# When the expert loads are issued, how many result tiles there are, and which weights are loaded early, in a mixture-of-experts tail

## The chip, the cores and the metric

The kernel runs on one NeuronCore of a Trainium2 chip. The metric is the time of one execution on the device in microseconds (us). The median of three timed runs of the kernel before is 1958.4 us (1953.89 to 1959.58).

## What is computed

Sixteen sequences of 256 rows of 512 numbers go through four residual stages: a cross attention, a base matrix product with low-rank experts, a second attention with 8 heads, and last a mixture of 64 experts with the 8 best experts for each row and a capacity of 256 rows for each expert. The change touches the last stage:

```python
logits = xf @ router_weight
probs = jax.nn.softmax(logits.astype(jnp.float32), axis=-1)
topw, topi = jax.lax.top_k(probs, TOPK)
topw = topw / topw.sum(axis=-1, keepdims=True)
...
xe = jnp.zeros((E, CAP, d), x.dtype).at[se, pos].set(xf[tok], mode='drop')
h = jax.nn.silu(jnp.einsum('ecd,edi->eci', xe, gate_proj)) * jnp.einsum('ecd,edi->eci', xe, up_proj)
ye = jnp.einsum('eci,eid->ecd', h, down_proj)
contrib = jnp.where(valid[:, None], ye[se, posc], 0.0) * flat_w[order][:, None]
out = jnp.zeros((m, d), x.dtype).at[tok].add(contrib)
```

## The kernel before

The program has two parts. In the first, a written-out order interleaves the attention stages of the 16 sequences on all engines; at its end each row of a sequence is sent by GpSimd's indirect DMAs (line 1405) to the slots of its experts in a DRAM array, `slot_rows`, 128 rows and one of the 8 choices at a time. The first part ends when the last of these sends has landed.

In the second part the 64 experts are worked through, each in two units of 128 slots. Unit u belongs to expert u // 2. All engines walk over the same index t, each with its own lead:

- TensorE at t: transposes of the slot rows of unit t + 3 (line 762), the gate and up products of unit t + 2 (lines 773 to 775), the transposes of the hidden values of unit t + 1 (line 784), the down product of unit t (lines 795 to 797). Every product is made of three, from high and low parts of its factors.
- ScalarE at t: the high part of the transposed rows (line 988), silu (994), the high part of the hidden values (1000), the scaled result of unit t into the tile `y_slots` (`ye`, line 1008, in `down`), then half of an expert's `gate_up_hi` (1018) three experts ahead.
- VectorE at t: the low parts (lines 1300, 1314, 1321) and at even t the high part of the down weights, two experts ahead (1331).
- GpSimd: at odd t `add_rows(t // 2)`, two indirect DMAs (line 1454) that add the two result tiles of an expert to their rows of `out_rows` in DRAM; at even t `split_down((t + 4) // 2)`, the low part of an expert's down weights (line 1444). `add_rows(e)` waits until the additions of expert e - 1 have landed, since two experts may add to the same row.
- SyncE (SP) issues the loads: `load_weights(e)` (`gate_up`, 768 KB, and `down`, 384 KB, lines 493 and 496) and `load_rows(e)` (`x_slots`, 577 KB, line 504). There are five buffers (NB) of weights and of rows. `load_rows(e)` for e of 5 or more waits until the additions of expert e - 5 have landed, since these read their row numbers from the same buffer. In its main loop SP issues, for expert e, the weights of expert e + 4 and then the rows of expert e + 3.

There are two result tiles, one for each parity of the expert, so `down` of expert e waits until the additions of expert e - 2 have landed. The semaphores `added` count 32 for each expert. In GpSimd's order `split_down(e + 3)`, which raises `dn_lo_ok` to e + 4, stands directly behind `add_rows(e)`.

Of the kernel before, what the change touches and what calls it, by code (L numbers as in the profile page):

```python
# [7 lines left out]
ALU = mybir.AluOpType  # L8
ACT = mybir.ActivationFunctionType
# [6 lines left out]
P = 128  # L16
# [118 lines left out]
def build(nc, a, out, slots_dram, dims):  # L135
    B, HALF, T, L, NHEAD, DQ, NE, NEXP, CAP, TOPK, NRANK = (
        dims[k] for k in ("B", "HALF", "T", "L", "NHEAD", "DQ", "NE", "NEXP", "CAP", "TOPK", "NRANK"))
# [14 lines left out]
    NX = 4  # L152
    NB = 5
    NW = 3
    BC = NHEAD * C

    tensor_order = schedule(dims, TENSOR, TENSOR_TAIL, TENSOR_MAX, TENSOR_OUT, ("key", "score", "weighted"))
# [12 lines left out]
    for _, ev in tensor_order:  # L170
        stage = bank_stage(ev)
        if stage and stage not in use:
            i = min((read_last[i], taken[i], i) for i in range(3))[2]
            use[stage] = 5 + i, taken[i]
            taken[i] += 1
            read_last[i] = read_at[stage]

    stack = ExitStack()
    with stack:
        def sem(name):  # L180
            return stack.enter_context(nc.semaphore(name))

        def sb(name, shape, dt=F32, on=stack):
            return on.enter_context(nc.sbuf_tensor(name, shape, dt))

        psum = [stack.enter_context(nc.psum_tensor(f"bank{i}", [P, 512], F32)) for i in range(8)]
# [12 lines left out]
        sent = [sem(f"sent{i}") for i in range(2)]  # L199
# [52 lines left out]
        added = [sem(f"added{i}") for i in range(2)]  # L252
# [4 lines left out]
        dn_lo_ok = sem("dn_lo_ok")  # L257
# [101 lines left out]
        xe = [sb(f"x_slots{i}", [P, 2, ROW]) for i in range(NB)]  # L359
        gu_hi, gu_lo = ([sb(f"gate_up_{part}{i}", [P, C, 2 * INNER], F32R) for i in range(NW)] for part in ("hi", "lo"))  # L360
        dn_hi, dn_lo = ([sb(f"down_{part}{i}", [IC, 2, T], F32R) for i in range(NW)] for part in ("hi", "lo"))
        xt_hi, xt_lo = ([sb(f"x_slots_t_{part}{i}", [P, C, P], F32R) for i in range(3)] for part in ("hi", "lo"))
        act_g = [sb(f"silu{i}", [P, INNER]) for i in range(2)]
        hid = [sb(f"hidden{i}", [P, INNER]) for i in range(2)]
        ht_hi, ht_lo = ([sb(f"hidden_t_{part}{i}", [IC, 2, P], F32R) for i in range(2)] for part in ("hi", "lo"))
        ye = [sb(f"y_slots{i}", [P, 2, T]) for i in range(2)]


        N_WEIGHTS = 16 * (3 * HALF + 10)
# [2 lines left out]
        U = 2 * NEXP  # L372

        full_a = [BC * B // 2] * 4 + [0] + taken

        def sent_before(b):

            return 16 * HALF * TOPK * (b // 2)
# [4 lines left out]
        def expert_slots(e_):  # L383
            return slots_dram[e_ * CAP:(e_ + 1) * CAP, :].rearrange("(c p) w -> p c w", p=P)
# [4 lines left out]
        def _(e):  # L389
            w = Waits(e)  # L390
# [31 lines left out]
            def stacks_free(b):  # L422
                if b >= 2:
                    n = BC * (b - 1)
                    w.wait_ge(full[0], n // 2)
# [63 lines left out]
            def load_weights(e_):  # L489
                i, k = e_ % NB, e_ // NB  # L490
                if k:
                    w.wait_ge(gu_lo_ok, 2 * (e_ - NB) + 2)
                e.dma_start(gu[i][:, :, :], a["gate_up"][e_]).then_inc(weights_of[i], 16)
                if k:
                    w.wait_ge(dn_lo_ok, e_ - NB + 1)
                e.dma_start(dn[i][:, :, :], a["down"][e_]).then_inc(weights_of[i], 16)

            def load_rows(e_):
                i, k = e_ % NB, e_ // NB
                if k:  # L500
                    u = 2 * (e_ - NB) + 1
                    w.wait_ge(free[6 + u % 2], full_a[6 + u % 2] + u // 2 + 1)
                    w.wait_ge(added[(e_ - NB) % 2], 32 * ((e_ - NB) // 2 + 1))
                e.dma_start(xe[i][:, :, :], expert_slots(e_)).then_inc(rows_of[i], 16)

            load_weights(0)
            for i in range(2):
                w.wait_ge(sent[i], sent_before(B))
            for e_ in range(NB - 2):
                load_rows(e_)  # L510
                load_weights(e_ + 1)
            for t in range(0, U, 2):
                if t // 2 + NB - 1 < NEXP:
                    load_weights(t // 2 + NB - 1)
                if t // 2 + NB - 2 < NEXP:
                    load_rows(t // 2 + NB - 2)
            for i in range(2):
                w.wait_ge(added[i], 32 * (NEXP // 2))
            w.wait_ge(slots_filled, 16 * (NEXP + 1))
# [2 lines left out]
        def _(e):  # L522
            w = Waits(e)

            def take(bank, n):

                if n:
                    w.wait_ge(free[bank], n)
# [109 lines left out]
            def score_chunk(n):  # L638
                b, head, c, h = place(n)
                take(2 + n % 2, n // 2)  # L640
                if n % BC == 0:
                    w.wait_ge(q_in[b % 2], 16 * 3 * HPH * (b // 2 + 1))
# [59 lines left out]
            def dispatch(b, what, _):  # L702
                if what in ("x0", "x1"):
                    k = int(what[1])
                    w.wait_ge(rows_ok, 2 * b + k + 1)
                    bank, done = turn_of("disp", what, b)
                    for c in range(C):
                        m = e.transpose(bank[:, c * P:(c + 1) * P], rows[b % 2][:, k, c * P:(c + 1) * P], ident[:, :])
                    m.then_inc(done, 1)
                elif what == "route":  # L710
                    for k in range(HALF):
                        bank, n = use["disp", f"x{k}", b]
                        w.wait_ge(free[bank], n + 1)
                    bank, done = turn_of("disp", what, b)
                    for k in range(HALF):
                        for c in range(C):
                            m = e.matmul(bank[:, k * NEXP:(k + 1) * NEXP], x_t4[:, k, c, :], route_w[:, c, :],
                                         start=c == 0, stop=c == C - 1)
                    m.then_inc(done, 1)
                elif what == "place":  # L720
                    w.wait_ge(mask_ok, b + 1)
                    if b:
                        w.wait_ge(seen_ok, b)
                    bank, done = turn_of("disp", what, b)
                    for k in range(HALF):
                        dst = bank[:, k * NEXP:(k + 1) * NEXP]
                        e.matmul(dst, below[:, :], mask[:, k, :], start=True, stop=False)
                        for kk in range(k):
                            e.matmul(dst, ones[:, :], mask[:, kk, :], start=False, stop=False)
                        m = e.matmul(dst, ones[:, :], seen[:, :], start=False, stop=True)  # L730
                    m.then_inc(done, 1)
# [33 lines left out]
            def up(u):  # L765
                e_ = u // 2
                nw = e_ % NW
                bk = psum[2 + u % 2]
# [18 lines left out]
            def down(u):  # L787
                e_ = u // 2
                nw = e_ % NW
                bk = psum[6 + u % 2]  # L790
# [20 lines left out]
        def _(e):  # L811
            w = Waits(e)
# [190 lines left out]
            def down(u):  # L1003
                e_, s = divmod(u, 2)
                w.wait_ge(full[6 + u % 2], full_a[6 + u % 2] + u // 2 + 1)
                if e_ >= 2:
                    w.wait_ge(added[e_ % 2], 32 * (e_ // 2))
                e.activation(ye[e_ % 2][:, s, :], psum[6 + u % 2][:, :], ACT.Copy,  # L1008
                             scale=xe[e_ % NB][:, s, T + 1 + e_:T + 2 + e_]).then_inc(free[6 + u % 2], 1)

            def split_gate_up(e_, half):
                i, nw = e_ % NB, e_ % NW
                cs = slice(half * C // 2, (half + 1) * C // 2)
                w.wait_ge(weights_of[i], 32 * (e_ // NB + 1))
                if e_ >= NW:
                    u = 2 * (e_ - NW) + 1
                    w.wait_ge(full[2 + u % 2], full_a[2 + u % 2] + u // 2 + 1)
                e.copy(gu_hi[nw][:, cs, :], gu[i][:, cs, :]).then_inc(gu_hi_ok, 1)  # L1018
# [14 lines left out]
        def _(e):  # L1033
            w = Waits(e)
# [255 lines left out]
                    dispatch(*ev[1:])  # L1290

            w.wait_ge(slots_ok, B)
            for i in range(2):
                w.wait_ge(sent[i], sent_before(B))

            def turn(u):
                w.wait_ge(xt_hi_ok, u + 1)
# [48 lines left out]
        def _(e):  # L1346
            w = Waits(e)
# [99 lines left out]
            def add_rows(e_):  # L1447
                i, u = e_ % NB, 2 * e_
                w.wait_ge(free[6], full_a[6] + e_ + 1)
                w.wait_ge(free[7], full_a[7] + e_ + 1)  # L1450
                if e_:
                    w.wait_ge(added[(e_ - 1) % 2], 32 * ((e_ - 1) // 2 + 1))
                for q in range(2):
                    e.indirect_dma_start(  # L1454
                        out=out, out_offset=bass.IndirectOffsetOnAxis(ap=xe[i][:, q, T:T + 1].bitcast(U32), axis=0),
                        in_=ye[e_ % 2][:, q, :], in_offset=None, compute_op=ALU.add).then_inc(added[e_ % 2], 16)

            for t in range(-6, U):
                if t >= 0 and t % 2:
# [48 lines left out]
```

## Time and profile before

| | |
|---|---|
| median of the timed runs | 1958.4 us |
| the profiled execution | 1951.5 us |
| its span | 1949.6 us |
| last send issued | 1278.6 us into the span |
| first additions issued by GpSimd | 1306.8 us |
| last expert's additions issued | 1941.8 us |
| TensorE busy, whole span | 86% |
| VectorE, ScalarE, GpSimd busy | 61%, 51%, 47% |

The span counts from the first instruction to the last one of the profiled execution. A row of the timeline gives start, duration, engine, line, operation and tiles, and in brackets how long the engine had stood idle before and what released it. A wait for several things is put down to the one that the profile saw last, so that a name in brackets can be wrong where two things end close together.

### The profile page before, as it was taken

What the parts mean: (1) busy time and instruction counts of PE and PEld (TensorE: products, weight loads), DVE (VectorE), ACT (ScalarE), POOL (GpSimd) and SP (SyncE); (2) the same over time, 40 slices, a digit from 0 to 9 for tenths busy, and PEclk for the clock granted to TensorE, in tenths of its full rate; (3) what the DMA queues carried; (4) which work ended last, traced back from release to release, by engine and by line L of the source; (5) the groups of instructions that cost most, each with busy time, mean ns of one, the idle gap of its engine ahead of it and who ended that gap; (6) DMA issues with size and microseconds to landing.
All of it is one profiled execution on the core that took longest, in us unless ns stands there. A gap on an engine that the chain in (4) does not pass through costs nothing.

```text
span 1949.6 us, 25985 instructions
## 1 busy us (share of the span) xinstructions
PE 1678.9 (86%) x8672; PEld 1086.1 (56%) x8672; DVE 1195.8 (61%) x2644; ACT 996.1 (51%) x1970; POOL 922.4 (47%) x880
## 2 busy tenths in 40 slices
PE   4688999999999999999999988459888888888885
PEld 2343454544554544555455443258777777777775
DVE  2465677777777777677777765346555555554553
ACT  3345656656655655655665635135444444444443
POOL 1121225445446436436535536645555555555555
PEclk9889999999999999999999989679999999999998
DMA  9767325345344343332332220168888888888885
GB/s 335 241 232 250 87 53 165 107 137 162 106 141 140 113 112 115 103 104 80 95 87 71 58 65 25 37 219 230 225 216 227 233 227 223 215 229 225 222 222 89
DMA packets 138194, 303.31 MB, mean 156 GB/s; under 512 B 26617, under 2 KB 27513, under 8 KB 138062
## 3 DMA queue, kind: packets, MB, share of 16 engines
q1 hardware_dynamic: 99150, 230.23, 39.1%
q0 software_dynamic: 38912, 71.43, 15.3%
q8 instruction: 69, 1.13, 0.2%
q14 instruction: 63, 0.52, 0.1%
HBM read 132.60 MB, written 155.91 MB: 148 GB/s over the span
## 4 chain that ended last, share of the span: by engine, by line
PE 37%; DMA 25%; POOL 14%; DVE 9%; issue 7%; ACT 5%; SPq 3%; POOLq 0%; ACTq 0%
DMA out_rows<-y_slots,x_slots 23%; POOL out_rows L1454 5%; POOL slot_rows L1405 5%; PE bank L652 5%; PE bank L644 4%; PE bank L665 4%; PE bank L625 4%; POOL p_sum L1393 3%; PE bank L688 3%; ACT y_slots L1008 2%; SPq L410 2%; PE bank L598 2%; PE bank L566 2%; PE bank L681 2%; PE bank L612 1%
## 5 line engine op out<-in xcount | busy, mean ns | idle before, releaser
L1174 DVE TENSOR_REDUCE max_col<-bank 128x1 f32<-128x512 f32 x512 | 345.4, 684 | 216.2 <-PE bank L644 213.7
L929 ACT ACTIVATE p_t<-bank 128x512 f32<-128x512 f32 x512 | 298.2, 597 | 283.2 <-PE bank L652 264.0
L1405 POOL DMA_INDIRECT slot_rows<-row,slot_i x256 | 266.5, 1041 | 330.3 <-DVE slot_i L1273 261.6
L1454 POOL DMA_INDIRECT out_rows<-y_slots,x_slots x128 | 201.1, 1571 | 291.1 <-ACT y_slots L1008 260.4
L652 PE MATMUL bank<-q_stack,k_stack 98*128 98x512 f32 x512 | 275.7, 540 | 5.5 <-ACT p_t L929 5.1
L773 PE MATMUL bank<-gate_up_hi,x_slots_t_hi 128*128 128x384 f32 x512 | 187.4, 366 | 87.3 <-DVE x_slots_t_lo L1300 87.2
L1300 DVE TENSOR_TENSOR x_slots_t_lo<-bank,x_slots_t_hi 128x512 fp32r<-128x512 f32 x128 | 88.5, 691 | 251.2 <-ACT x_slots_t_hi L988 244.7
L644 PE MATMUL bank<-k_stack,q_stack 96*128 96x512 f32 x512 | 216.0, 424 | 19.2 <-DMA q_stack<-xn 16.5
L1393 POOL TENSOR_TENSOR p_sum<-p_t 128x512 f32<-128x512 f32 x128 | 162.6, 1278 | 139.5 <-ACT p_t L929 138.4
L1008 ACT ACTIVATE y_slots<-bank,x_slots 128x512 f32<-128x512 f32 x128 | 88.7, 694 | 268.7 <-DMA out_rows<-y_slots,x_slots 257.6
L1444 POOL TENSOR_TENSOR down_lo<-down,down_hi 96x1024 fp32r<-96x1024 f32 x64 | 188.6, 2947 | 18.2 <-DVE down_hi L1331 18.2
L775 PE MATMUL bank<-gate_up_hi,x_slots_t_lo 128*128 128x384 f32 x512 | 176.2, 344 | 0.0
L774 PE MATMUL bank<-gate_up_lo,x_slots_t_hi 128*128 128x384 f32 x512 | 175.3, 342 | 0.0
L652 PEld LDWEIGHTS bank<-q_stack,k_stack 98*128 98x128 f32 x512 | 98.4, 193 | 133.2 <-issue 107.0
L1321 DVE TENSOR_TENSOR gate_up_lo<-gate_up,gate_up_hi 128x768 fp32r<-128x768 f32 x128 | 149.6, 1170 | 23.7 <-DMA slot_rows<-row,slot_i 23.7
L773 PEld LDWEIGHTS bank<-gate_up_hi,x_slots_t_hi 128*128 128x128 f32 x512 | 98.6, 193 | 100.8 <-DVE x_slots_t_lo L1300 100.5
L665 PE MATMUL bank<-p_t,v_t 128*32 128x512 f32 x1024 | 139.5, 617 | 0.0
L644 PEld LDWEIGHTS bank<-k_stack,q_stack 96*128 96x128 f32 x512 | 100.5, 197 | 60.1 <-DMA q_stack<-xn 24.1
L625 PE MATMUL bank<-base_w,x_t 128*128 128x512 f32 x256 | 126.7, 608 | 0.0
L1018 ACT CAST gate_up_hi<-gate_up 128x768 fp32r<-128x768 f32 x128 | 106.3, 831 | 36.3 <-DMA down<-in_down 36.3
L795 PE MATMUL bank<-down_hi,hidden_t_hi 96*128 96x512 f32 x256 | 113.6, 444 | 0.0
L762 PE MATMUL bank<-ident,x_slots 128*128 128x128 f32 x512 | 77.7, 274 | 29.7 <-DMA x_slots<-slot_rows 29.7
(174 smaller groups left out, 3269.1 us busy)
## 6 DMA issues: line engine op xcount, KB each, us to landing
gate_up<-in_gate_up SPq DMA_DIRECT2D x64, 768.0 KB, 5.7
slot_rows<-row SPq DMA_DIRECT2D x64, 577.0 KB, 8.6
x_slots<-slot_rows SPq DMA_DIRECT2D x64, 577.0 KB, 3.9
k_stack<-prob SPq DMA_DIRECT2D x192, 128.0 KB, 2.4
down<-in_down SPq DMA_DIRECT2D x64, 384.0 KB, 7.3
q_stack<-x_t SPq DMA_DIRECT2D x128, 128.0 KB, 2.3
x<-in_x SPq DMA_DIRECT2D x16, 512.0 KB, 4.2
ctx<-in_ctx SPq DMA_DIRECT2D x16, 512.0 KB, 3.8
```

The costliest lines, as they stand in the source:

```text
L625: e.matmul(bank[:, :], x_t[:, k, c, :], base_w[:, c, :], start=c == 0, stop=False)
L644: e.matmul(psum[2 + n % 2][:, :], q_st[b % 2][0:SK, head, c * P:(c + 1) * P], k_st[b % 2][0:SK, head, :], start=True, stop=True).then_inc( ...
L652: e.matmul(psum[n % 2][:, :], k_st[b % 2][0:SKM, head, j * P:(j + 1) * P], q_st[b % 2][0:SKM, head, :], start=True, stop=True).then_inc(fu ...
L665: m = e.matmul(psum[4][h * DQ:(h + 1) * DQ, :], v_t[b % 3][:, j, head + h, :], p_t[step % 2][:, h, :], start=j == 0, stop=j == C - 1)
L773: e.matmul(bk[:, 0:2 * INNER], xt_hi[u % 3][:, c, :], gu_hi[nw][:, c, :], start=c == 0, stop=False)
L775: m = e.matmul(bk[:, 0:2 * INNER], xt_lo[u % 3][:, c, :], gu_hi[nw][:, c, :], start=False, stop=c == C - 1)
L929: e.activation(p_t[step % 2][:, h, :], psum[n % 2][:, :], ACT.Exp, scale=SCALE).then_inc(free[n % 2], 1)
L1174: e.tensor_reduce(max_col[quad % 2][:, c, h:h + 1], psum[2 + n % 2][:, :], X, ALU.max, negate=True).then_inc(free[2 + n % 2], 1)
L1393: e.tensor_tensor(p_sum[:, h, :], p_t[(step - 1) % 2][:, h, :], p_t[step % 2][:, h, :], ALU.add).then_inc(p_sum_ok, 1)
L1405: e.indirect_dma_start(out=slots_dram, in_=rows[b % 2][:, k, :], in_offset=None, out_offset=bass.IndirectOffsetOnAxis(ap=slot_i[b % 2][:, ...
L1444: e.tensor_tensor(dn_lo[nw][:, :, :], dn[i][:, :, :], dn_hi[nw][:, :, :].bitcast(F32), ALU.subtract).then_inc(dn_lo_ok, 1)
L1454: e.indirect_dma_start(out=out, out_offset=bass.IndirectOffsetOnAxis(ap=xe[i][:, q, T:T + 1].bitcast(U32), axis=0), in_=ye[e_ % 2][:, q, : ...
```

## The change

There are three result tiles instead of two, so `down` of expert e waits for the additions of expert e - 3. SP loads the weights of experts 0 to 4 before it waits for the last sends (before: of expert 0 alone), then the rows of experts 0 to 3. In its main loop it waits, for expert e, until `dn_lo_ok` is e + 4, which GpSimd signals at the end of the `split_down` that stands behind `add_rows(e)`; only then it issues the weights of expert e + 5 and the rows of expert e + 4. VectorE no longer waits for the last sends before its work on the experts.

```diff
+    NY = 3
...
-        ye = [sb(f"y_slots{i}", [P, 2, T]) for i in range(2)]
+        ye = [sb(f"y_slots{i}", [P, 2, T]) for i in range(NY)]
...
-            load_weights(0)
+            for e_ in range(NB):
+                load_weights(e_)
             for i in range(2):
                 w.wait_ge(sent[i], sent_before(B))
-            for e_ in range(NB - 2):
+            for e_ in range(NB - 1):
                 load_rows(e_)
-                load_weights(e_ + 1)
-            for t in range(0, U, 2):
-                if t // 2 + NB - 1 < NEXP:
-                    load_weights(t // 2 + NB - 1)
-                if t // 2 + NB - 2 < NEXP:
-                    load_rows(t // 2 + NB - 2)
+            for e_ in range(NEXP):
+                w.wait_ge(dn_lo_ok, min(e_ + NB - 1, NEXP))
+                if e_ + NB < NEXP:
+                    load_weights(e_ + NB)
+                if e_ + NB - 1 < NEXP:
+                    load_rows(e_ + NB - 1)
...
-                if e_ >= 2:
-                    w.wait_ge(added[e_ % 2], 32 * (e_ // 2))
-                e.activation(ye[e_ % 2][:, s, :], psum[6 + u % 2][:, :], ACT.Copy,
+                if e_ >= NY:
+                    w.wait_ge(added[(e_ - NY) % 2], 32 * ((e_ - NY) // 2 + 1))
+                e.activation(ye[e_ % NY][:, s, :], psum[6 + u % 2][:, :], ACT.Copy,
...
             w.wait_ge(slots_ok, B)
-            for i in range(2):
-                w.wait_ge(sent[i], sent_before(B))
...
-                        in_=ye[e_ % 2][:, q, :], in_offset=None, compute_op=ALU.add).then_inc(added[e_ % 2], 16)
+                        in_=ye[e_ % NY][:, q, :], in_offset=None, compute_op=ALU.add).then_inc(added[e_ % 2], 16)
```

The program of the SyncE queue at the start of the second part, before. `gate_up` and `down` are an expert's weights, `x_slots` its rows, `sent0` and `sent1` the landing of the sends.

```order
L493 DMA gate_up<-in_gate_up 128x1536 [waits out_in1,out_in2,out_in0,out_in3,out_rstd_ok,slots_ok]
L496 DMA down<-in_down 96x1024
L504 DMA x_slots<-slot_rows 128x2x577 [waits sent1,sent0]
L493 DMA gate_up<-in_gate_up 128x1536
L496 DMA down<-in_down 96x1024
L504 DMA x_slots<-slot_rows 128x2x577
L493 DMA gate_up<-in_gate_up 128x1536
```

The same place of the changed kernel, whose lines are numbered one higher.

```order
L497 DMA down<-in_down 96x1024
L494 DMA gate_up<-in_gate_up 128x1536
L497 DMA down<-in_down 96x1024
L505 DMA x_slots<-slot_rows 128x2x577 [waits sent1,sent0]
L505 DMA x_slots<-slot_rows 128x2x577 x3
L494 DMA gate_up<-in_gate_up 128x1536 [waits gu_lo_ok,dn_lo_ok]
L497 DMA down<-in_down 96x1024
L505 DMA x_slots<-slot_rows 128x2x577
```

Ten weight loads now stand ahead of the wait for the sends, four row loads directly behind it, and the fifth row load stands behind a wait on `dn_lo_ok`.

The SyncE queue in the main loop, before: the weights wait for their buffer, the rows for the additions of five experts earlier.

```order
L493 DMA gate_up<-in_gate_up 128x1536 [waits gu_lo_ok]
L496 DMA down<-in_down 96x1024 [waits dn_lo_ok]
L504 DMA x_slots<-slot_rows 128x2x577 [waits added1,bank_free7]
L493 DMA gate_up<-in_gate_up 128x1536 [waits gu_lo_ok]
L496 DMA down<-in_down 96x1024 [waits dn_lo_ok]
```

And in the changed kernel.

```order
L494 DMA gate_up<-in_gate_up 128x1536 [waits gu_lo_ok,dn_lo_ok]
L497 DMA down<-in_down 96x1024
L505 DMA x_slots<-slot_rows 128x2x577 [waits added0,bank_free7]
L494 DMA gate_up<-in_gate_up 128x1536 [waits gu_lo_ok,dn_lo_ok]
L497 DMA down<-in_down 96x1024
```

Before, the wait that holds the queue stands at the rows, and the weights follow it freely. Now it stands at the weights, with a higher value of `dn_lo_ok` than the buffer needs, and the rows are the last of the three.

## Rows read from the trace of the kernel before

**Rows 1.** Busy time by stretch: start:end, length, engines, PEclk (granted clock), DMA share, GB/s.

```profile
1264.00:1278.00 14.00, 0.00 (x0) 0.00 (x0) 0.00 (x0) 0.96 (x2) 10.65 (x12) 0.50 0.04 5
...
1500.00:1600.00 100.00, 82.50 (x467) 73.55 (x467) 53.45 (x90) 47.50 (x100) 55.37 (x30) 1.00 0.83 227
1700.00:1800.00 100.00, 89.21 (x470) 79.57 (x468) 49.82 (x87) 46.00 (x96) 52.69 (x29) 0.93 0.82 220
```

**Rows 2.** Waits from 1340 to 1890: engine, line, releaser, us in total, times, longest.

```profile
ACT y_slots L1008 <- DMA out_rows<-y_slots,x_slots: 238.7, 54, 5.9
...
PE bank L773 <- DVE x_slots_t_lo L1300: 79.6, 47, 3.1
```

**Rows 3.** Timeline of one expert from 1499.9 us.

```profile
1499.90 0.38 SPq L504 DMA_DIRECT2D x_slots<-slot_rows  x1
1500.62 1.55 POOL L1454 DMA_INDIRECT out_rows<-y_slots,x_slots  x1 [4.38 <-ACT y_slots L1008]
1500.84 0.43 SPq L496 DMA_DIRECT2D down<-in_down  x1
1502.48 1.55 POOL L1454 DMA_INDIRECT out_rows<-y_slots,x_slots  x1 [0.30 <-issue]
...
1510.93 1.55 POOL L1454 DMA_INDIRECT out_rows<-y_slots,x_slots  x1 [4.47 <-ACT y_slots L1008]
```

**Rows 4.** Chain that ended last, final experts: start, us, what.

```profile
1926.62 1.55 POOL out_rows L1454
...
1936.17 4.88 DMA out_rows<-y_slots,x_slots
...
1941.12 0.71 issue
1941.83 1.55 POOL out_rows L1454
```

**Rows 5.** Timeline of the first experts, 1301 to 1319 us.

```profile
1306.78 1.62 POOL L1454 DMA_INDIRECT out_rows<-y_slots,x_slots  x1 [1.92 <-ACT y_slots L1008]
1310.59 3.00 POOL L1444 TENSOR_TENSOR down_lo<-down,down_hi 96x1024 fp32r<-96x1024 f32 x1
...
1305.27 0.69 ACT L1008 ACTIVATE y_slots<-bank,x_slots 128x512 f32<-128x512 f32 x1 [1.02 <-PE bank L797]
1313.49 0.69 ACT L1008 ACTIVATE y_slots<-bank,x_slots 128x512 f32<-128x512 f32 x1 [1.00 <-PE bank L797]
1317.63 0.69 ACT L1008 ACTIVATE y_slots<-bank,x_slots 128x512 f32<-128x512 f32 x1 [1.00 <-PE bank L797]
```

**Rows 6.** DMA queues by packets, MB, share; 1500 to 1505, every queue.

```profile
q1 hardware_dynamic: 384, 1.27, 77.1%
```

**Rows 7.** The same queues from 1507 to 1510 us.

```profile
q0 software_dynamic: 243, 0.43, 80.0%
```

**Rows 8.** GB/s in 40 slices of 1926 to 1941 us, without loads.

```profile
GB/s 0 0 0 0 0 0 0 87 76 109 180 169 120 87 66 147 180 142 33 0 0 0 0 0 0 0 0 44 82 93 115 186 148 115 98 131 164 169 55 0
```

**Rows 9.** DMA queues, and issue to landing, 1290 to 1950 us.

```profile
q1 hardware_dynamic: 32666, 109.35, 51.1%
q0 software_dynamic: 18432, 33.56, 29.6%
...
down<-in_down SPq DMA_DIRECT2D x59, 384.0 KB, 7.2
out_rows<-y_slots,x_slots POOLq DMA_INDIRECT x128, 7.9
```

**Rows 10.** Timeline of the start of the second part.

```profile
1257.38 0.36 SPq L493 DMA_DIRECT2D gate_up<-in_gate_up  x1
1280.91 0.38 SPq L504 DMA_DIRECT2D x_slots<-slot_rows  x1
1284.98 1.94 PE L762 MATMUL bank<-ident,x_slots 128*128 128x128 f32 x8 [29.74 <-DMA x_slots<-slot_rows]
1288.41 0.83 ACT L1018 CAST gate_up_hi<-gate_up 128x768 fp32r<-128x768 f32 x1 [23.45 <-DMA down<-in_down]
1290.51 0.69 PE L773 MATMUL bank<-gate_up_hi,x_slots_t_hi 128*128 128x384 f32 x1 [3.59 <-DVE x_slots_t_lo L1300]
```

## The prediction

> **What bounds the kernel now.** I read the page first. Its slices show that the second part, from about 1285 us on, has TensorE busy and the DMA engines at eight to nine tenths together, so neither share alone names the bound. The stretches [rows 1] say the same in numbers: from 1500 to 1600 TensorE is busy 82.5 of 100 us and the DMA engines 83%. Something else holds both back a little. The table of waits [rows 2] names it: ScalarE stood 238.7 us for the landing of additions, in 54 waits over some 54 experts, once an expert; TensorE's 79.6 us of waits behind it are for a tile that ScalarE was late with.
>
> The timeline of one expert [rows 3] shows the whole ring. Call A(e) the start of GpSimd's first add of expert e. At 1499.9 an earlier expert's additions have landed. Three things start on that one event: SP issues the next rows (and, to 1500.84, the weights), ScalarE writes the blocked result tile, and 0.7 us later GpSimd issues the next additions. GpSimd's release is put down to ScalarE, which ended just then. I don't believe this name: at the end of the kernel, where no result is written in between, the same 0.71 us lie between the landing and the issue [rows 4]. It is GpSimd's own delay, so the ring is landing, 0.7 us, two issues 1.86 us apart, and the flight of the second, about 7.7 us: 10.31 us from 1500.62 to 1510.93. The result tile is not on it. From the first additions at 1306.78 to the last at 1941.83 there are 63 steps in 635.05 us [rows 4, 5], 10.08 each.
>
> Why is the flight so long? Without loads it is 4.88 us [rows 4], with them the median of both adds is 7.9 [rows 9]. By queue: in 1500 to 1505, though the first add was issued at 1500.62, the only queue with packets is the loads' q1, 384 of them [rows 6]; the additions' q0 carries its packets after 1505, 243 of them in 1507 to 1510 [rows 7]. The additions stand behind 1.77 MB of loads that were issued less than a microsecond before them. So the same landing triggers a transfer that delays the next landing.
>
> **What TensorE could do.** While it was not held up, results came 4.14 us apart (1313.49 and 1317.63 [rows 5]). I take 4.13 for a unit, 8.26 for an expert. DMA work for an expert is 660 us × (51.1 + 29.6)% / 64 = 8.3 us, of which 3.05 for the additions and 5.3 for the loads [rows 9]. Both floors are near 8.3, against 10.08 now.
>
> **The change, part by part.**
>
> *Loads behind the issue of the additions.* SP now waits for the down split behind add_rows(e). In the stretch that TensorE paced, the additions of expert 0 were issued at 1306.78 and the split ran from 1310.59 for 3.00 us [rows 5]: it ends at A + 6.8. Additions that meet no loads need 1.86 + 4.88 = 6.7 us, so those of expert e have landed when the loads start. The next ones come up against the tail of these loads. Loads issued at A + 6.8 start to move about 1.0 us later (the engines filled from about 1501 on after 1499.9 in the ring above, an estimate from [rows 3, 6]) and need 5.3 us of work: until A + 13.1. The next additions at, say, A + 9.2 move 2.0 us after their issue in the unloaded case [rows 4, 8], so from A + 11.2; they wait 1.9 us, then have 3.05 us of work, and land near their own + 7.0. With 0.7 us of delay this ring takes 7.7 us. It stops being the bound.
>
> Whether the additions really stand behind the loads matters here. The rows say so: no packet of q0 in the 4.4 us after its issue [rows 3, 6], where a lone add, issued at 1926.62, moved its first bytes in the eighth slice of 0.375 us, at about 1928.6, so after 2.0 [rows 4, 8]. The Trainium skill, DMA: Bandwidth & Descriptors, section "Queues, rings and completion order", says otherwise: each DMA engine goes round robin between the queues that it has work for, a packet at a time. By that rule the tail of the loads would come later than in the terms above, and the time would be that of the first rival below, some 30 us more; the packets of [rows 6] do not look like it.
>
> *What is late next: the rows.* The rows of expert e + 4 are now the last of three loads issued at A(e) + 6.8; before, they were issued at A(e) - 0.7. The same three loads took from 1499.90 to 1500.84 + 7.2 = 1508.0, 8.1 us [rows 3, 9]; I take 8.0, though part of it was shared with additions. So the rows land at A(e) + 14.8. TensorE transposes them three units ahead of their down product. In TensorE's order the transposes of unit 2e + 8 open step t = 2e + 5; from there to the end of the down product of unit 2e + 9 are five steps, 5 × 4.13 = 20.65 us. The additions follow that end by about 1.5 us (result at 1305.27, additions at 1306.78, [rows 5]; 1.55 with the handover). So
>
> A(e+4) - A(e) = 14.8 + 20.65 + 1.55 = 37.0 us, or 9.25 an expert.
>
> Unheld, four experts would take 33.0, so TensorE will stand about 4 us in every fourth expert, or a share of it in each. The weights of expert e + 5 go ahead of the rows in the same queue and are wanted by ScalarE only at t = 2e + 4, with some slack; they do not add to it. I count them at nothing; the cover is the wait for the rows.
>
> *Three result tiles.* On the ring above the tile is not a link, so its price is nothing in the sum; with two tiles, though, ScalarE would stop at t = 2e until the additions of e - 2 landed, and TensorE's lead would be gone. It is the cover that lets the rows be the bound. It costs no instruction.
>
> *Weights early.* From 1264 to 1278, during the last sends, the DMA engines are 4% busy at 5 GB/s [rows 1]. Five experts' weights are 5.9 MB; at the 1.77 MB in 5.3 us of [rows 9] about 18 us, from 1257.38 [rows 10] to about 1276, before the rows are issued at 1280.91. They are hidden. Before, ScalarE had to split the weights of expert 1, landed only at 1288.41, before it got to the first transposed rows, and the first product began at 1290.51 though its transposes began at 1284.98 [rows 10]. Now that product starts after half the transposes (1.0), one ScalarE and one VectorE pass over 128x512 (each about the 0.69 of the one in [rows 5]) and handovers: about 1287.4. That is 3.1 us gained, once. VectorE's dropped wait is part of this and worth nothing else.
>
> **The sum.** Fifteen groups of four, 15 × 37.0 = 555, and three last steps at 8.26, 25: 580 us where 635 were. With 3.1 at the start the profiled execution's 1951.5 us becomes 1951.5 - 55 - 3 = 1893. The timed runs had a median 7 us above it (and one at 1953.9), so I say 1895. The granted clock, 0.93 in 1700 to 1800 [rows 1], was covered by waits; 7% of the 20.65 us is 1.4 us a group, some 10 us if half of the groups meet it. I leave it to the range, since the waits for rows come on top of it only in part.
>
> **Bounds of the unknown.** The delay of the rows: at best the split starts when the second add is in the queue (in the ring at A + 2.9, end A + 5.9) and the loads run alone, about 7.0: 12.9 instead of 14.8, so 35.1 a group and 1864. At worst of this case the landing takes 9.5: 38.5, and 1915.
>
> **Rivals.**
>
> *The queues take turns.* If the additions share the engines with the rest of the loads instead of standing behind them, the rows land up to 1.9 us later: 38.9 a group, 583.5 + 25 = 608.5, and 1922 us. Against it stand the packets of [rows 6]. The rule of the Trainium skill named above (DMA: Bandwidth & Descriptors) is this case. Chance 0.15.
>
> *Everything is in time.* If the rows landed by A + 10.8 the group would be at TensorE's 33.0: 63 × 8.26 = 520, and 1834 us. It needs rows 4 us sooner than the terms above. 0.1.
>
> *The ring stays.* If the additions still flew 7.7 us, because some loads are always in flight, only the 3 us of the start are won: 1948 us. The loads of one expert would have to cover every moment, but they work 5.3 us out of 10. 0.05.
>
> *Slower: the loads stand still while additions fly.* If the engines stopped the loads' tail for the whole flight of the next additions, 4.9 us, instead of the other way round, the rows would land at A + 19.7: 41.9 a group, 628.5 + 25 = 653.5, and 1967 us. The point from which it decides is 40.9 a group, rows at A + 18.7. For it speaks only that rows are now the last load, with 7.5 us less lead. 0.08.
>
> **The numbers.** The forecast has 0.57, and 0.05 lie between the cases. The range takes the forecast's 1864 to 1915, the turn-taking case and a little below: 1858 to 1930, which leaves out the two at the upper end and the one at 1834. A measurement tells this kernel from no change at about 0.3%, 6 us. Faster 0.87, the same 0.05, slower 0.08.
>
> **What would show it.** Right: the second add's flight falls from 7.7 to between 5 and 6.5 us; q0 carries packets within about 2 to 4 us of its issue; additions are 9.2 us apart; TensorE's wait at the transposes (line 762) is on the row load, some 4 us each fourth expert, and ScalarE's wait for landed additions is near nothing; the first product starts at 1287. Wrong: flights that stay over 7 us, or no wait of TensorE for rows (then the loads were hidden), or waits of more than 6 us (then the lead lost is worth more than I say).

## The result, and the profile after

The changed kernel takes 2031.4 us (median of 4 runs, 2023.55 to 2032.22) against 1956.1 for the kernel before in the same comparison: the ratio is 1.0377, with a 95% interval of 1.0342 to 1.0412. It is slower by 3.8%. I had forecast 1895 us, with a range of 1858 to 1930, and put 0.08 on slower.

Two stretches by the same view as [rows 1], the first during the last sends, the second in the middle of the second part: start and end, length, busy time of TensorE, its weight loads, VectorE, ScalarE and GpSimd, then the granted clock, the DMA share and GB/s.

```profile
1264.00:1278.00 14.00, 0.00 (x0) 0.00 (x0) 2.43 (x3) 2.40 (x3) 10.68 (x11) 0.50 1.04 305
...
1500.00:1600.00 100.00, 76.27 (x390) 68.55 (x388) 44.93 (x76) 42.63 (x84) 56.93 (x27) 0.86 0.82 203
```

The early weights fill 1264 to 1278 as meant. From 1500 to 1600 TensorE is busy less (76 us against 82 in [rows 1]) and at a lower granted clock (0.86 against 1.00). The waits from 1340 to 1890, to be held against [rows 2]:

```profile
POOL out_rows L1456 <- ACT y_slots L1012: 185.7, 30, 11.9
...
PE bank L766 <- DMA x_slots<-slot_rows: 104.7, 27, 7.4
...
ACT gate_up_hi L1022 <- DMA down<-in_down: 42.8, 24, 3.1
...
POOL out_rows L1456 <- DMA out_rows<-y_slots,x_slots: 27.2, 16, 2.5
```

ScalarE's 238.7 us of waits for landed additions are gone, and GpSimd waits for them only 27 us. TensorE now stands 105 us for the rows (line 766 is 762 of before), in 27 waits over some 48 experts: about every second one, 3.9 us each, not every fourth. One turn of the chain that ended last tells why. This is the chain in order of time: start, duration, what.

```profile
1514.09 1.55 POOL out_rows L1456
1515.65 0.31 issue
1515.95 2.56 POOL out_rows L1456
1518.52 2.44 POOL down_lo L1446
...
1520.97 0.33 SPq L494
...
1521.35 0.42 SPq L497
...
1521.87 7.52 DMA x_slots<-slot_rows
...
1529.43 1.11 PE bank L766 x4
1530.55 0.32 PE bank L777
...
1534.81 0.35 PE bank L799
...
1536.36 0.70 ACT y_slots L1012
...
1537.09 0.71 issue
1537.80 1.55 POOL out_rows L1456
```

From one expert's additions at 1514.09 the chain goes over the down split (it ends near A + 6.9), both weight issues, the row load (landed at 1529.4, A + 15.3), TensorE's transposes, its products and the result into the additions at 1537.80. These are not four experts later but two: the timeline has one other pair of additions between them.

```profile
1514.09 1.55 POOL L1456 DMA_INDIRECT out_rows<-y_slots,x_slots  x1 [8.65 <-ACT y_slots L1012]
1522.35 1.55 POOL L1456 DMA_INDIRECT out_rows<-y_slots,x_slots  x1 [1.41 <-ACT y_slots L1012]
1537.80 1.55 POOL L1456 DMA_INDIRECT out_rows<-y_slots,x_slots  x1 [8.65 <-ACT y_slots L1012]
```

So 23.7 us are spent for two experts here, where two of the kernel before take 20. Over the steady part, from 1331.12 to 1998.69 us, 58 steps take 667.6 us, 11.5 each against 10.08 before. From the first additions (1308.55) to the last (2022.31) it is 713.8 us against 635.05 in [rows 4, 5]: 78.7 us more, nearly all of the 80.7 us between the two profiled executions (2032.2 and 1951.5).

The step behind the wait is also longer than I counted. Two stretches of TensorE, the first from the landing of rows at 1505.9, with the columns as above.

```profile
1505.90:1511.00 5.10, 5.08 (x19) 4.95 (x19) 0.69 (x1) 0.69 (x2) 0.00 (x0) 0.50 1.03 296
1511.00:1515.00 4.00, 4.00 (x25) 3.65 (x24) 2.06 (x4) 2.50 (x5) 0.91 (x1) 0.99 0.33 117
```

After 4.6 us without work TensorE comes back at a granted 0.50, its 1.2 GHz level, and gets through 19 matmuls in 5.1 us; then it is at 0.99 and gets through 25 in 4.0. From the landing at 1529.4 to the start of the result at 1536.36 pass 6.9 us where I took 4.13.

### The profile page after: what moved, and what is told of

It reads as the page before. It is cut to its first block, busy times and chain, and to the rows that moved or that the text cites. A ratio compares the mean times of both kernels' runs of the same rounds, so it can differ in the third digit from the quotient of the medians.

```text
span 2030.3 us, 26043 instructions
## 1 busy us (share of the span) xinstructions
PE 1721.8 (85%) x8672; PEld 1127.5 (56%) x8672; DVE 1188.7 (59%) x2644; ACT 1014.6 (50%) x1970; POOL 974.4 (48%) x880
## 4 chain that ended last, share of the span: by engine, by line
PE 44%; POOL 18%; DMA 14%; DVE 9%; issue 8%; ACT 4%; SPq 4%; POOLq 0%; ACTq 0%; DVEq 0%
DMA x_slots<-slot_rows 11%; POOL out_rows L1456 6%; POOL slot_rows L1407 5%; PE bank L656 4%; PE bank L648 4%; PE bank L629 4%; PE bank L669 4%; POOL down_lo L1446 3%; POOL p_sum L1395 3%; PE bank L692 2%; SPq L411 2%; PE bank L777 2%; PE bank L778 2%; PE bank L779 2%; PE bank L602 2%
## 5 line engine op out<-in xcount | busy, mean ns | idle before, releaser
L1456 POOL DMA_INDIRECT out_rows<-y_slots,x_slots x128 | 253.5, 1981 | 318.9 <-ACT y_slots L1012 231.3
L1395 POOL TENSOR_TENSOR p_sum<-p_t 128x512 f32<-128x512 f32 x128 | 162.6, 1278 | 139.4 <-ACT p_t L933 138.4
L766 PE MATMUL bank<-ident,x_slots 128*128 128x128 f32 x512 | 91.8, 309 | 160.6 <-DMA x_slots<-slot_rows 160.3
L777 PE MATMUL bank<-gate_up_hi,x_slots_t_hi 128*128 128x384 f32 x512 | 203.4, 397 | 0.5 <-DVE x_slots_t_lo L1302 0.5
L778 PE MATMUL bank<-gate_up_lo,x_slots_t_hi 128*128 128x384 f32 x512 | 189.4, 370 | 0.0
L779 PE MATMUL bank<-gate_up_hi,x_slots_t_lo 128*128 128x384 f32 x512 | 189.2, 370 | 0.0
L766 PEld LDWEIGHTS bank<-ident,x_slots 128*128 128x128 f32 x512 | 69.6, 157 | 187.7 <-DMA x_slots<-slot_rows 145.5
L1323 DVE TENSOR_TENSOR gate_up_lo<-gate_up,gate_up_hi 128x768 fp32r<-128x768 f32 x128 | 135.9, 1062 | 7.5 <-ACT gate_up_hi L1022 7.5
L648 PEld LDWEIGHTS bank<-k_stack,q_stack 96*128 96x128 f32 x512 | 100.7, 197 | 60.0 <-DMA q_stack<-xn 23.6
L998 ACT ACTIVATE silu<-bank 128x192 f32<-128x192 f32 x128 | 42.2, 330 | 156.2 <-PE bank L779 156.2
```

What stands on the lines that cost most here:

```text
L648: e.matmul(psum[2 + n % 2][:, :], q_st[b % 2][0:SK, head, c * P:(c + 1) * P], k_st[b % 2][0:SK, head, :], start=True, stop=True).then_inc( ...
L777: e.matmul(bk[:, 0:2 * INNER], xt_hi[u % 3][:, c, :], gu_hi[nw][:, c, :], start=c == 0, stop=False)
L778: e.matmul(bk[:, 0:2 * INNER], xt_hi[u % 3][:, c, :], gu_lo[nw][:, c, :], start=False, stop=False)
L779: m = e.matmul(bk[:, 0:2 * INNER], xt_lo[u % 3][:, c, :], gu_hi[nw][:, c, :], start=False, stop=c == C - 1)
L1395: e.tensor_tensor(p_sum[:, h, :], p_t[(step - 1) % 2][:, h, :], p_t[step % 2][:, h, :], ALU.add).then_inc(p_sum_ok, 1)
L1456: e.indirect_dma_start(out=out, out_offset=bass.IndirectOffsetOnAxis(ap=xe[i][:, q, T:T + 1].bitcast(U32), axis=0), in_=ye[e_ % NY][:, q, ...
```

## The experiments

Theory 1 was formed on this trace: the rows close a ring over two experts, since TensorE works in order and the transposes of unit 2e + 8 stand ahead of the down product of unit 2e + 5, which is expert e + 2's. Theory 2, the rival: the loads behind the issue cost DMA throughput, whichever of them is first. And how much of it is the low clock was open.

**Rows first.** The rows are issued ahead of the weights.

```diff
                 w.wait_ge(dn_lo_ok, min(e_ + NB - 1, NEXP))
+                if e_ + NB - 1 < NEXP:
+                    load_rows(e_ + NB - 1)
                 if e_ + NB < NEXP:
                     load_weights(e_ + NB)
-                if e_ + NB - 1 < NEXP:
-                    load_rows(e_ + NB - 1)
```

> The changed kernel, but SyncE issues the rows of expert e + 4 ahead of the weights of expert e + 5, both still behind the down split. Theory 1 (the rows land too late: a ring over two experts, additions of e, down split, row load behind two weight loads, transposes that block the down product of e + 2, additions of e + 2): the rows land some 3.5 us sooner, at A + 11.5 instead of A + 15.3, TensorE no longer waits for rows, and the clock stays up. ScalarE then meets the weights that land at about A + 15, its ring over two experts is 15 + 3 + 1.4 = 19.4 us, 9.7 an expert: about 1920 to 1940 us. Theory 2 (the loads behind the issue cost DMA throughput or the additions' flight, whichever load is first): no change, 2031 us.

Measured: 1899.3 us, ratio 0.9716 (0.9693 to 0.9738). A swap of two lines turns 3.8% slower into 2.8% faster; the time is 20 us under the range. A miss in size: the additions are 9.15 us apart on average, for the 9.7 that I expected. The chain shows the ring that I expected next.

```profile
1509.29 1.73 POOL out_rows L1456
...
1513.93 2.43 POOL down_lo L1446
...
1516.38 0.37 SPq L505
...
1517.30 7.47 DMA down<-in_down
...
1526.59 0.59 ACT y_slots L1012
...
1527.93 1.79 POOL out_rows L1456
```

ScalarE, in order too, waits for the landed `down` before it can write the result of two experts later: 18.6 us for two, 9.3 an expert. It is not always met (the chain around 1700 goes from additions to additions), so the mean is below that. Theory 2 falls, since the same bytes stand behind the same wait.

**Six row buffers.** The order of the changed kernel (weights, then rows) is kept, but a sixth buffer lets the rows be those of expert e + 5. The places that index the row buffers change with it.

```diff
+    NR6 = 6
...
-        xe = [sb(f"x_slots{i}", [P, 2, ROW]) for i in range(NB)]
+        xe = [sb(f"x_slots{i}", [P, 2, ROW]) for i in range(NR6)]
...
-            for e_ in range(NB - 1):
+            for e_ in range(NR6 - 1):
                 load_rows(e_)
...
-                if e_ + NB - 1 < NEXP:
-                    load_rows(e_ + NB - 1)
+                if e_ + NR6 - 1 < NEXP:
+                    load_rows(e_ + NR6 - 1)
```

> The changed kernel with a sixth row buffer: the loads still stand behind the down split, weights of e + 5 first, rows last, but the rows are those of expert e + 5 instead of e + 4. Nothing leaves or moves but which expert's rows are fetched. If the ring over two experts is the cause, one more expert of lead makes it a ring over three (15.3 + 6.9 + 1.4 = 23.6, 7.9 an expert at most), it binds no longer, and ScalarE's ring on the weights (A + 14 + 3 over two) or the DMA engines at 8.3 to 8.7 do: 0.945 to 0.97 of the kernel before. If it is the throughput or the order of the transfers that costs, the ratio stays near 1.038.

Measured: 1898.1 us, ratio 0.9701 (0.9672 to 0.9731), at the upper edge of the forecast. TensorE's wait for rows does not appear among the larger waits any more. This isolates the lead: the bytes and their order are the same, the rows take 7.6 us to land as before (7.3 in the changed kernel), and only the distance to their use is one expert longer. What the kernel runs into next is not what I had expected: the chain from 1494 to 1528 goes from additions to additions, with flights of 5.3 to 7.0 us, and they are 9.2 us apart on average.

**Two tiles.** The changed kernel with `NY = 2`.

```diff
-    NY = 3
+    NY = 2
```

> The changed kernel with two result tiles instead of three. Theory 1: at 23 us for two experts the additions of expert e - 2 have landed long before the result of expert e is written, so the third tile is idle: 2031 us within 0.5%. If the third tile mattered in this kernel, it would be slower still, 2060 us or more.

Measured: 2027.2 us, ratio 1.0364 (1.0322 to 1.0406), the same as with three. The third tile has no part in the loss, and gives nothing here.

**No wait on the issue.** Each landing of additions again releases rows and then weights, as before the change; three tiles and early weights stay. One difference is left: the weights behind a landing are those of one expert earlier than in the kernel before, so they have one expert less of lead.

```diff
-                w.wait_ge(dn_lo_ok, min(e_ + NB - 1, NEXP))
-                if e_ + NB < NEXP:
-                    load_weights(e_ + NB)
                 if e_ + NB - 1 < NEXP:
                     load_rows(e_ + NB - 1)
+                if e_ + NB < NEXP:
+                    load_weights(e_ + NB)
```

> The changed kernel without the wait on the down split in SyncE's main loop: rows of e + 4, then weights of e + 5, each as soon as its buffer is free, as before the change; three result tiles and early weights stay. Theory 1: all the loss is in the moved loads, the ring of additions at 10.2 us comes back, and the start gives 2.5 us: 1952 to 1956 us against 1956 before. A rival that puts the loss on the early weights or on the third tile expects more than 1980 us here.

Measured: 1960.3 us, ratio 1.0014 (1.0002 to 1.0027). The loss is in the moved loads alone. The additions are 10.16 us apart on average, against 10.08 before the change. But the old ring is back only in part. Around 1500 the chain runs over the weights instead:

```profile
1493.91 6.64 DMA down<-in_down
...
1502.37 0.60 ACT y_slots L1011
1502.96 0.27 SPq L505
...
1503.95 7.21 DMA down<-in_down
```

ScalarE waits for `down` before it writes a result, SP's next row load waits for that result, and the next weights stand behind that row load: 10.0 us an expert. Around 1700 part of it goes from additions to additions again. So this run shows where the loss lies, not what three tiles alone would do with the old loads. The 2.5 us of the start, which I had hoped to see, don't show; the median is 4 us above the range, and the 63 steps from the first to the last additions took 639.8 us against 635.05.

**Warm.** Extra transposes fill most of TensorE's wait.

```diff
                 take_b(u % 2, u)
+                if s == 0 and e_ >= NB - 1:
+                    for _ in range(20):
+                        e.transpose(psum[u % 2][:, 0:P], ident[:, :], ident[:, :])
                 w.wait_ge(rows_of[i], 16 * (e_ // NB + 1))
```

> The changed kernel with 20 extra transposes of the identity (about 2.2 us at full clock) on TensorE ahead of each expert's wait for its rows, from expert 4 on, into the bank that the next transposes overwrite; the results don't change. If the low clock behind each wait is what makes the step behind it 6.9 instead of 4.1 us, the idle time becomes too short for the clock to fall, the ring over two experts goes from 23.0 to about 21 us, and the time to 1970 to 1985 us although TensorE has 140 us more of work. If the clock costs nothing on the ring, the extra work is hidden in the wait or adds: 2031 us or more.

Measured: 1979.2 us, ratio 1.0122 (1.0103 to 1.0141). More work on the engine that waits makes the kernel 52 us faster than the changed one.

```profile
1500.00:1600.00 100.00, 99.50 (x653) 92.74 (x652) 47.83 (x84) 47.78 (x94) 63.50 (x29) 1.00 0.88 216
```

The clock is at 1.00 and the additions are 10.4 us apart. TensorE is full now: 8.26 us and the 2.19 us that the 20 transposes take in this trace make 10.45, so the ring itself may be a little below 10.4. The low clock costs at least the 52 us.

**The mark.** Three kernels shorten the delay of the loads instead. GpSimd sets a mark directly behind its additions and SP waits for that, so the loads need not wait for the split.

```diff
                         in_=ye[e_ % NY][:, q, :], in_offset=None, compute_op=ALU.add).then_inc(added[e_ % 2], 16)
+                e.memset(mark[:, e_:e_ + 1], 0.0).then_inc(add_issued, 1)
...
-                w.wait_ge(dn_lo_ok, min(e_ + NB - 1, NEXP))
+                w.wait_ge(add_issued, e_ + 1)
```

The first issues the rows first, as above.

> The changed kernel with a one-column memset on GpSimd directly behind each expert's two additions; SyncE's loop waits for this mark instead of the down split, and issues rows first, then weights. The loads start about 3.5 us sooner after the additions (A + 3.4 instead of A + 6.9). Theory 1: ScalarE's ring over two experts, 18.6 us with the wait on the split, falls to 15 and binds no longer; what is left is the ring of additions (first in the DMA engines, but now partly in flight with the loads of their own expert) or TensorE's 8.26: 8.5 to 8.9 us an expert, 1860 to 1885 us. If the additions must have landed before the loads start (the point of waiting for the split), their flight goes back to 7.5 and the time to 1900 to 1955.

Measured: 1886.5 us against 1971.8 us of the kernel before, run beside it on the same chip, ratio 0.9587 (0.9543 to 0.963). It beats both kernels. As measured that is 1.5 us above the range; scaled to the 1956 us of the first comparison it is 0.9587 × 1956 = 1875 us, inside it. In this trace a longer first part goes with the longer time: the last send is issued at 1298.6 us here, at 1282.8 in the changed kernel. Its stretches and its largest wait on GpSimd:

```profile
1500.00:1600.00 100.00, 96.74 (x554) 87.24 (x554) 58.31 (x105) 57.85 (x119) 72.68 (x46) 1.00 1.00 271
1600.00:1700.00 100.00, 98.05 (x566) 89.06 (x565) 59.37 (x107) 57.93 (x118) 75.77 (x48) 1.00 1.01 265
```

```profile
POOL out_rows L1458 <- DMA out_rows<-y_slots,x_slots: 113.3, 55, 3.6
```

TensorE is busy 97% and the DMA engines all of the time, so both are near the floors of 8.3 us that I had worked out. Neither is what the chain shows, though. It goes from additions to additions, each first one waiting for the landing of those before:

```profile
1504.77 6.24 DMA out_rows<-y_slots,x_slots
...
1511.07 0.71 issue
1511.78 1.56 POOL out_rows L1458
```

From first to last the additions are 8.69 us apart on average, inside the expected 8.5 to 8.9. What is left is the old ring, in the stretch from 1496 to 1528 with flights of 5.3 to 6.2 us in place of 7.7.

The second has two result tiles.

> The same with two result tiles. At 8.5 us an expert the additions of e - 2 landed some 2 to 3 us before the first result of e is written, so the third tile gives nothing: within 0.5% of the kernel with three. If it is needed in the fastest version, this one is 1% or more slower.

Measured: 0.9572 (0.9514 to 0.963), the same. Even in the fastest version the third tile gives nothing.

The third issues the weights first and the rows last.

> The mark again, but weights first and rows last, as in the changed kernel. Theory 1 by its formula: rows land at A + 3.4 + 0.9 + 7.5 to 9 = A + 11.8 to 13.3, the ring over two experts is that plus a step of 4.13 (the idle time before it is short enough for the clock to stay) and 1.44: 17.4 to 18.9, 8.7 to 9.4 an expert, 1870 to 1915 us, slower than with the rows first. If only the order of rows and weights mattered and not the delay, it would stay above 1980.

Measured: ratio 1.0097 (1.0065 to 1.0129). A miss: faster than the changed kernel, as the shorter delay must make it, but far above the expected 1870 to 1915 us. The chain shows both terms.

```profile
1514.64 1.57 POOL out_rows L1458
...
1519.06 0.13 POOL mark L1461
...
1520.14 8.02 DMA x_slots<-slot_rows
...
1528.20 0.75 PE bank L768 x4
1528.95 0.32 PE bank L779
```

The mark comes at A + 4.6, not 3.4, and the rows land at A + 13.5. That alone would be (13.5 + 4.13 + 1.44) / 2 = 9.5 an expert. But TensorE still stood long enough (3.6 us at 1506.48 in this trace) to come back at 0.32 us for a matmul that takes 0.17 at full clock. The next kernel tests just that: the same with 10 extra transposes.

```diff
+                if s == 0 and e_ >= NB - 1:
+                    for _ in range(10):
+                        e.transpose(psum[u % 2][:, 0:P], ident[:, :], ident[:, :])
                 w.wait_ge(rows_of[i], 16 * (e_ // NB + 1))
```

> The kernel with the mark and the rows last (1.0097 of before, against a forecast of 0.96 to 0.98 that took the step behind the wait at 4.13 us) with 10 extra transposes of the identity, 1.1 us at full clock, ahead of each expert's wait for rows; the results don't change. If the miss was the low clock behind a wait of 3.6 us, the step falls from 6.7 to 4.1, the ring to 13.6 + 4.1 + 1.4 = 19.2 or 9.6 an expert, and the ratio to 0.98 to 0.99. If the clock was not it, the ratio stays at 1.01 or rises.

Measured: 0.9912 (0.9884 to 0.9941). The expected range ended just below, at 0.99, inside the interval; two experts take 19.9 us (additions at 1505.26 and 1525.17) for the 19.2 of the formula. So the clock was 0.0185 of the miss. Most of the rest lies in the rows, which land at A + 14.05 in this trace where at most 13.3 had been expected.

**Rows at landing.** The rows are issued when the additions of e - 1 have landed, as before the change, and only the weights stand behind the split.

```diff
+                if e_ + NB - 1 < NEXP:
+                    load_rows(e_ + NB - 1)
                 w.wait_ge(dn_lo_ok, min(e_ + NB - 1, NEXP))
                 if e_ + NB < NEXP:
                     load_weights(e_ + NB)
-                if e_ + NB - 1 < NEXP:
-                    load_rows(e_ + NB - 1)
```

> The changed kernel with the rows of e + 4 issued as soon as the additions of e - 1 have landed (as before the change) and only the weights of e + 5 behind the down split. Theory 1: TensorE finds its rows; the additions have 0.58 MB ahead of them instead of 1.77, which costs them some 1.5 us of flight (6.5 instead of 4.9, ring 9.1); ScalarE's ring over two experts is A + 6.9 + 6.5 + 3.1 = 16.5. So about 9.1 us an expert, 1890 to 1905 us, near the kernel with rows first behind the split.

Measured: 1918.8 us, 0.9727 (0.9702 to 0.9752) of the 1971.8 us of the kernel before run beside it; scaled to the 1956 us of the first comparison, that is 1903 us, inside the range, where the time as measured lies 14 us above it. Its last send is issued at 1303.7 us, 21 later than in the changed kernel, and the additions are 9.22 us apart on average for the expected 9.1. Its chain from 1499.5 to 1525.6 is additions to additions, with flights of 5.4 to 7.95 us.

## Why the prediction was wrong

**What bounded the kernel before** was read rightly as far as the runs go. With the loads out of the way of the additions' start and rows in time (rows first, six buffers, mark), the kernel gains 2.8 to 4.1%. Even the fastest version is bound by that ring, shortened to 8.7 us, a little above the two floors.

**The flight of the additions** fell as forecast: the median from issue to landing is 5.9 us in the changed kernel, 7.9 before ([rows 9]). The additions also stand behind loads as the argument from [rows 6] had it, and don't take turns with them. An add of the changed kernel was issued at 1522.35, just behind three loads issued from 1520.97 to 1521.87. These are the queue rows of three single microseconds, 1526, 1527 and 1529:

```profile
q1 hardware_dynamic: 121, 0.29, 98.9%
```

```profile
q1 hardware_dynamic: 134, 0.29, 79.3%
q0 software_dynamic: 28, 0.06, 31.0%
```

```profile
q0 software_dynamic: 110, 0.21, 113.6%
q1 hardware_dynamic: 1, 0.00, 0.1%
```

In each microsecond from 1522 to 1526 q0 has nothing, so nothing for 4.6 us after its issue, against 2.0 for a lone add; I had said 2 to 4 us. Counted over the packets of this trace, for the first addition of each of experts 2 to 59: where a load was issued at most 2.1 us before (29 of them), q0's first packet came 3.6 to 5.4 us after the issue; where the last load was more than 6 us old (21), it came after 2.1; for the 8 between, after 2.1 to 2.5. What holds q0 back no run shows.

**The delay of the rows** was right to 0.5 us: forecast A + 14.8, measured A + 15.3.

**The step that failed is the ring of the rows**, "from there to the end of the down product of unit 2e + 9 are five steps", and so "A(e+4) - A(e) = 37.0". The wait for the rows of expert e + 4 stands at the head of step 2e + 5. Everything behind it on TensorE waits with it, and the last thing in that same step is the down product of unit 2e + 5, whose result completes expert e + 2. The ring closes there, one step after the landing: 14.8 + 4.13 + 1.55 = 20.5 us for two experts, 10.24 each. I followed the data of the late rows to their own expert and forgot what they block on the way. With the right ring the terms of the prediction give about the 10.08 us an expert of the kernel before, some 1958 us, already outside my range. Six row buffers, which change only the distance to the use, show that it was this ring, and the swap of the order agrees.

**The weights at nothing** was the same mistake once more, "they do not add to it". Here rows hide it; with the rows first ScalarE's wait for the landed `down` closes its own ring over two experts, 9.3 us an expert, as much as the 9.25 of my forecast.

**A second term was missing**: the clock behind a wait. I had left the clock to the range, as something that the waits cover. It is the waits that bring it down: the step behind the wait took 6.9 us, not 4.13, which makes 15.3 + 6.9 + 1.4 = 23.6 of the ring, against 23.7 measured in the turn shown and 23.0 on average. This is what turned no change into 3.8% slower; with extra transposes in the wait the changed kernel gets 52 us of it back, and the one with the mark and the rows last 1.9%. My slower rival had a price for late rows (the decision point at A + 18.7), but by the wrong ring; by the right one the kernel was at its decision point at A + 14.8.

**The start.** The first product began 2.5 us after the first transposes (1289.20 and 1291.69) where it was 5.5 in [rows 10]: 3.0 gained there, as forecast. But the rows were not free to come as soon as before. From SP's first weight load to its first row load pass 24.25 us (1260.93 to 1285.18) where 23.53 passed in [rows 10], 0.7 us more. One send is now issued beside VectorE's cast of the early weights (1270.11 to 1270.79) and takes 1.66 us where its neighbours take 0.97:

```profile
1269.38 1.66 POOL L1407 DMA_INDIRECT slot_rows<-row,slot_i  x1 [0.30 <-issue]
```

So 2.4 us are left at the first product, and 1.8 at the first additions (47.6 us after that weight load for 49.4); no comparison of whole kernels resolves that.

**The third tile** at nothing was right, but it was not the cover I called it: left out, it changes nothing, in the changed kernel (1.0364 for 1.0377) and in the fastest one (0.9572 for 0.9587).

## What to carry to other kernels

When a load is made later, ask first what stands behind the waiting instruction on its in-order engine, and close the ring at the nearest result that it blocks, not at the result that the data belong to. Put the load that an engine wants next ahead of the ones that are wanted later: here two lines in SP's order decide between 3.8% slower and 2.8% faster. And look at the granted clock behind a wait of TensorE: here the step behind waits of 3.6 and 4.6 us took 2.6 to 2.8 us longer, and the prediction had priced the wait alone.

## What the runs showed of the hardware

After a wait of 4.6 us TensorE came back at a granted 0.50 for the next 5.1 us of work, and after one of 3.6 us at the same 0.32 us for a matmul that takes 0.17 at full clock; extra transposes in the wait, with nothing else changed, made the kernel 52 us faster.

The packets of GpSimd's indirect DMA started 3.6 to 5.4 us after its issue when SP had issued loads at most 2.1 us before it, and 2.1 us after its issue when the last load was more than 6 us old.

GpSimd's second indirect DMA of an expert took 2.56 us in the changed kernel where it took 1.55 in [rows 3]. VectorE's cast of the down weights lies inside it only in the changed kernel:

```profile
1515.95 2.56 POOL L1456 DMA_INDIRECT out_rows<-y_slots,x_slots  x1 [0.31 <-issue]
...
1517.01 0.68 DVE L1333 CAST down_hi<-down 96x1024 fp32r<-96x1024 f32 x1
```

Counted over the timelines: in the changed kernel the cast runs beside 61 of the 128 additions, which take 1.73 to 2.60 us (median 2.56); the other 67 take 1.55 to 1.62. In the kernel before it runs beside 3. The send of 1.66 us above is the same thing. The cast is not the only one: without the wait on the issue, 38 additions have no cast beside them but start while VectorE computes `gate_up_lo` from two tiles in SBUF, and their median is 1.94 us.

The Trainium skill, GPSIMD Engine Reference, section "Key points", says that GpSimd shares its interfaces to SBUF, the on-chip memory, with VectorE and contends with VectorE's instructions in a 2-port mode or with two inputs in SBUF. The counts agree with that; which mode the cast runs in no run shows, and no experiment moved the cast alone.
